# A macaron block: the sixteenth feed-forward's second matrix with one Strassen level of seven products, attention steps over twelve slots, square sums on ScalarE

## The reference

```
x = x + 0.5 * ffn(layernorm(x))
x = x + attention(layernorm(x))
x = x + 0.5 * ffn(layernorm(x))        # the same W1, W3, W2

ffn(x):   hidden = silu(x @ W1.T) * (x @ W3.T)      # 512 -> 2048
          hidden = fwht(hidden)                     # Walsh-Hadamard over 2048
          out = hidden @ W2.T                       # 2048 -> 512
attention(x): rmsnorm, q, k, v by a ternary matrix; 16 heads of 32;
          per chunk of 128 tokens: decayed causal scores, times v,
          plus q times a state carried from chunk to chunk;
          rmsnorm twice, ternary projection
```

## Time and profile before

| | |
|---|---|
| median of 3 runs | 2327.85 us (2327.58 to 2328.8) |
| span of the profiled execution | 2325.7 us |
| PE busy | 2319.4 us |
| DVE busy | 1245.2 us |
| ACT busy | 728.1 us |
| POOL busy | 113.1 us |
| matmuls recorded | 12687 |

### The profile page before, as it was taken

The page is one execution under the profiler, slowest core; times in us unless marked ns, Lnnn a source line. Parts: engine busy times, 40 slices in busy tenths (PEclk is TensorE's granted clock), DMA queues, the critical chain, the costliest instruction groups (busy, mean ns, idle before and its releaser), DMA issues.

```text
span 2325.7 us, 32208 instructions
## 1 busy us (share of the span) xinstructions
PE 2319.4 (100%) x12687; PEld 1105.1 (48%) x12687; DVE 1245.2 (54%) x2484; ACT 728.1 (31%) x1323; POOL 113.1 (5%) x106
## 2 busy tenths in 40 slices
PE   9999999999999999999999999999999999999999
PEld 5444444444444444444444444444444544444444
DVE  7678465655565446546553556545564455455312
ACT  7646133223322332233223322332233323331211
POOL 0290000000000000000000000000000000000000
PEclk9999999999999999999999999999999999999999
DMA  9866533331333214232241214321433124131200
GB/s 244 223 164 170 145 86 75 95 98 32 100 69 105 62 36 113 75 93 50 54 137 43 60 55 114 98 57 32 127 66 104 40 59 96 36 91 37 72 19 19
DMA packets 318086, 200.83 MB, mean 86 GB/s; under 512 B 250096, under 2 KB 274928, under 8 KB 314096
## 3 DMA queue, kind: packets, MB, share of 16 engines
q1 hardware_dynamic: 317504, 197.99, 33.1%
q10 hardware_dynamic: 432, 0.79, 0.1%
HBM read 87.04 MB, written 56.10 MB: 62 GB/s over the span
## 4 chain that ended last, share of the span: by engine, by line
PE 99%; DVE 1%; ACT 0%; DMA 0%; issue 0%; ACTq 0%; DVEq 0%
PE l_bank L1557 28%; PE d_bank L1577 28%; PE g_bank L1557 28%; PE a_bank L1621 4%; PE a_bank L1598 2%; PE a_bank L1676 2%; PE a_bank L1632 1%; PE a_bank L1660 1%; PE a_bank L1646 1%; PE a_bank L1614 1%; PE a_bank L1666 0%; PE a_bank L1662 0%; PE d_bank L1522 0%; DMA xin<-in_L_attn_x_dram 0%; PE a_bank L1522 0%
## 5 line engine op out<-in xcount | busy, mean ns | idle before, releaser
L1577 PE MATMUL d_bank<-w2t,work 128*128 128x512 f16 x2940 | 671.8, 379 | 0.0
L1236 DVE SCALAR_TENSOR_TENSOR work<-l_bank,l_scale,work 128x512 f32<-128x512 f32 x256 | 191.8, 749 | 482.4 <-PE l_bank L1557 482.1
L1577 PEld LDWEIGHTS d_bank<-w2t,work 128*128 128x128 f16 x2940 | 283.7, 98 | 328.7
L1557 PE MATMUL l_bank<-xt,w3t 128*128 128x512 f16 x1536 | 352.4, 379 | 0.0
L1557 PE MATMUL g_bank<-xt,w1t 128*128 128x512 f16 x1524 | 349.7, 379 | 0.0
L939 ACT CAST work<-work 128x512 f16<-128x512 f32 x232 | 143.3, 618 | 562.1 <-DVE work L1236 561.2
L1557 PE MATMUL g_bank<-work,w1t 128*128 128x512 f16 x1344 | 308.4, 379 | 0.0
L1557 PE MATMUL l_bank<-work,w3t 128*128 128x512 f16 x1344 | 308.3, 379 | 0.0
L920 ACT ACTIVATE work<-g_bank,g_scale 128x512 f32<-128x512 f32 x256 | 175.3, 685 | 354.2 <-PE g_bank L1557 351.4
L1557 PEld LDWEIGHTS l_bank<-xt,w3t 128*128 128x128 f16 x1536 | 148.8, 98 | 176.6
L1557 PEld LDWEIGHTS g_bank<-xt,w1t 128*128 128x128 f16 x1524 | 147.3, 98 | 171.9 <-issue 0.8
(11 more groups left out here) (256 smaller groups left out, 1881.4 us busy)
## 6 DMA issues: line engine op xcount, KB each, us to landing
work<-parts_dram SPq DMA_DIRECT2D x192, 128.0 KB, 2.8
x_dram<-work SPq DMA_DIRECT2D x16, 1024.0 KB, 4.2
work<-x_dram SPq DMA_DIRECT2D x11, 1024.0 KB, 6.9
parts_dram<-q_parts SPq DMA_DIRECT2D x32, 256.0 KB, 2.0
parts_dram<-k_parts SPq DMA_DIRECT2D x32, 256.0 KB, 2.2
norm_dram<-cent SPq DMA_DIRECT2D x32, 256.0 KB, 2.0
w2t<-in_L_ffn_W_dram SPq DMA_DIRECT2D x31, 256.0 KB, 3.6
xin<-in_L_attn_x_dram SPq DMA_DIRECT2D x7, 1024.0 KB, 7.4
```

The costliest lines, as they stand in the source:

```text
L1236: nc.vector.scalar_tensor_tensor(out=hfull, in0=l_bank[:], scalar=l_scale[:, j:j + 1], in1=gate, op0=ALU.mult, op1=ALU.mult).then_inc(hful ...
L1557: ins = nc.tensor.matmul(dst[:], wt[:, wp, k, P * j:P * (j + 1)], src[:, xp, k, :], start=(k == 0 and wp == xp), stop=(k == KT - 1 and wp ...
L1577: ins = nc.tensor.matmul(d_bank[t][:], parts[:, hp, P * t:P * (t + 1)], w2t[:, j, wp, :], start=(j == 0 and hp == wp), stop=(j == HT - 1 a ...
```

## The change

Numbers and layouts first. The constant `FAST = 15` names the first feed-forward that is done the new way, so it is the sixteenth alone. The token operands `xt` and `yt` are laid out in two halves of 256 tokens, so the ordinary gate and lin matmuls of all feed-forwards but n = 1 read their 512 tokens as two runs of 256. The hidden values are scaled by a further 1/4. `wproj` loses its own place: it is saved to DRAM during n = 1 (`projsave`) and loaded over the place of `qs` for each batch (`projload`, 8 slots ahead of `proj`); `qT`, `lam_t`, `ident` and others move into the work area.

In the sixteenth, `hgate` and `hlin` make hidden tiles p and p + 8 for 256 tokens into the two halves of a bank. VectorE forms the four 128 x 128 blocks (2 hidden tiles x 2 token tiles), and sums of them; with them there are seven left operands, `combos`. The seven right operands are blocks and sums of blocks of W2; the sums are made once, in the fifteenth feed-forward (`w2sums`), one of four into `w2t` itself, three into DRAM, from where they are streamed for each pair (`w2stream`). `hdown` multiplies, seven products of three matmuls with 256 columns. `hout` and `hend` combine the seven results and the residual on ScalarE, VectorE and GpSimd.

```diff
+                    for e, tile in enumerate((p, p + PAIRS)):
+                        for k in range(KT):
+                            for wp, xp in ((0, 0), (0, 1), (1, 0)):
+                                ins = nc.tensor.matmul(dst[:, HALF * e:HALF * (e + 1)], wt[:, wp, k, P * tile:P * (tile + 1)],
+                                                       f.x[:, s_half, xp, k, :], start=(k == 0 and wp == xp),
+                                                       stop=(k == KT - 1 and wp == 1))
...
+                elif step == "hdown":
+                    pe.wait_ge(lo_ready, tiles_before(n) + HT * s_half + 2 * p + 2)
+                    pe.wait_ge(w2_streamed[q % 2], 16 * (q // 2 + 1))
+                    products = ((0, w2t[:, p, :, left], d_bank[0], left, True),
+                                (4, extra[:, :, 2], d_bank[0], right, False),
+                                (6, extra[:, :, 0], d_bank[1], left, True),
+                                (3, w2t[:, p, :, right], d_bank[2], right, True),
+                                (1, extra[:, :, 1], d_bank[2], left, False),
+                                (2, w2t[:, p + PAIRS, :, left], d_bank[3], left, True),
+                                (5, w2t[:, p + PAIRS, :, right], d_bank[3], right, False))
+                        for hp, wp in ((0, 0), (0, 1), (1, 0)):
+                            ins = nc.tensor.matmul(bank_m[:, cols], combos[:, q % 2, hp, combo, :], weights[:, wp, :],
+                                                   start=(p == 0 and opens and hp == wp), stop=(p == PAIRS - 1 and hp == 1),
+                                                   skip_group_check=True)
```

The steps of the sixteenth, and where `w2sums` go:

```diff
+                if n == FAST - 1 and j >= 2 and j % 2 == 0:
+                    steps += [("w2sums", j // 2 - 1)]
+            if n == FAST - 1:
+                steps += [("w2sums", PAIRS - 1)]
...
+            for s_half in range(2):
+                for p in range(PAIRS):
+                    steps += [("hgate", (s_half, p)), ("w2stream", PAIRS * s_half + p)] + slots.get(slot, []) + [("hlin", (s_half, p))]
+                    if n == FAST and s_half == 0 and p == 0:
+                        steps += [("begin", n - 1), ("down", HT - 1)] + [("resid", t) for t in range(TT)] + [("begin", n)]
+                    steps += [("hlow", (s_half, p, 0))] + slots.get(slot + 1, []) + [("hlow", (s_half, p, 1))]
+                    if p:
+                        steps += [("hdown", (s_half, p - 1))] + slots.get(slot + 2, [])
+                    elif s_half:
+                        steps += [("hdown", (0, PAIRS - 1)), ("hout", 0)] + slots.get(slot + 2, [])
+                        steps += [("hend", 0), ("resid", 0), ("resid", 1)]
+            if last:
+                steps += [("hdown", (1, PAIRS - 1)), ("hout", 1), ("hend", 1), ("resid", 2), ("resid", 3)]
```

`w2sums` on GpSimd, ScalarE and VectorE:

```diff
+                    pool.wait_ge(d_step, steps_before(FAST - 1) + p + 1)
+                    if p:
+                        pool.wait_ge(w2_sum_lo, 2 * p)
+                    for half_h, j in enumerate((p, p + PAIRS)):
+                        ins = nc.gpsimd.tensor_tensor(wide[:, half_h], w2t[:, j, 0, :], w2t[:, j, 1, :], ALU.add)
+                    link(ins)
+                    link(nc.gpsimd.tensor_tensor(w2_sums[:, 0], w2_sums[:, 1], w2_sums[:, 0], ALU.subtract))
+                    link(nc.gpsimd.tensor_tensor(w2_sums[:, 1], w2_sums[:, 1], w2_sums[:, 3], ALU.subtract))
+                    link(nc.gpsimd.tensor_tensor(w2_sums[:, 3], w2_sums[:, 3], w2_sums[:, 0], ALU.subtract))
+                    nc.gpsimd.tensor_tensor(w2_sums[:, 2], w2_sums[:, 2], w2_sums[:, 3], ALU.subtract).then_inc(w2_differences, 1)
...
+                    act.wait_ge(w2_differences, p + 1)
+                    nc.scalar.copy(w2t[:, p, 0, HALF:D], w2_sums[:, 0]).then_inc(w2_sum_hi, 1)
+                    nc.scalar.copy(streamed[:, p % 2, 0], w2_sums[:, 1:4]).then_inc(w2_sum_hi, 1)
...
+                    nc.vector.tensor_tensor(w2t[:, p, 1, HALF:D], w2_sums[:, 0], w2t[:, p, 0, HALF:D], ALU.subtract).then_inc(w2_sum_lo, 1)
+                    nc.vector.tensor_tensor(streamed[:, p % 2, 1], w2_sums[:, 1:4], streamed[:, p % 2, 0],
+                                            ALU.subtract).then_inc(w2_sum_lo, 1)
```

Attention in slots, relative to a group's first slot `at`, and the batch's tail, relative to its last pv:

```diff
-                    add(slots, at - 6, [("q", (b, g))])
-                    add(slots, at - 5, [("qlow", (b, g)), ("k", (b, g))])
...
+                    add(slots, at, [("kv", (b, g)), ("score", (b, g, 0)), ("sclow", (b, g, 0)), ("state", (b, g))])
+                    add(slots, at + 2, [("score", (b, g, 1)), ("sclow", (b, g, 1))])
+                    add(slots, at + 3, [("pv", (b, g, 0))])
+                    add(slots, at + 4, [("score", (b, g, 2)), ("sclow", (b, g, 2))])
+                    add(slots, at + 5, [("pv", (b, g, 1))])
+                    add(slots, at + 6, [("score", (b, g, 3)), ("sclow", (b, g, 3))])
+                    add(slots, at + 7, [("pv", (b, g, 2))])
+                    add(slots, at + 9, [("pv", (b, g, 3))])
...
+                    add(slots, at - 7, [("q", (b, g))])
+                    add(slots, at - 6, [("qlow", (b, g))])
+                    add(slots, at - 5, [("k", (b, g))])
+                    add(slots, at - 3, [("qspread", (b, g)), ("kspread", (b, g))])
+                    end = at + 9
-                    add(slots, end + 11 + t, [("proj", (b, t))])
+                    add(slots, end + 9 + t, [("proj", (b, t))])
+                add(slots, end + 1, [("projload", b)])
-            for at, b in ((19, 3), (109, 4), (253, 5), (364, 6), (461, 7)):
+            for at, b in ((19, 3), (109, 4), (253, 5), (353, 6), (461, 7)):
```

```diff
-                    nc.vector.bn_stats(stat[:, t, :], x2[:, t, :]).then_inc(o_stats, 1)
+                    dve.wait_ge(o_stats, 2 * TT * a + squares_before(t, 0) + 1)
                     nc.vector.tensor_tensor(x2[:, t, :], x2[:, t, :], nw_row[:], ALU.mult).then_inc(o_scaled, 1)
-                    dve.wait_ge(o_scaled, TT * a + (t + 1))
-                    nc.vector.bn_stats(stat[:, TT + t, :], x2[:, t, :]).then_inc(o_stats, 1)
...
+                nc.scalar.activation(squares_out[:, i % 2], x2[:, t, :], ACT.Square, accum_out=sums).then_inc(o_stats, 1)
```

More of the change, by code:

```diff
@@ L289, in feed_forward @@
                 steps += slots.get(base + 3 * j + 2, [])
-                if n == 2 * B - 1 and j == 3:
-                    steps += [("back", batch)]
-            if n == 2 * B - 1:
-                return steps + [("down", HT - 1)] + finish
-            return steps + ([("back", batch)] if which == "ffn2" else [])
+                if n == FAST - 1 and j >= 2 and j % 2 == 0:
+                    steps += [("w2sums", j // 2 - 1)]
+            if n == FAST - 1:
+                steps += [("w2sums", PAIRS - 1)]
@@ L340, in attention_slots @@
                 for t in range(TT):
-                    add(slots, end + 11 + t, [("proj", (b, t))])
-                add(slots, end + 11 + TT, [("keep", b)])
+                    add(slots, end + 9 + t, [("proj", (b, t))])
+                add(slots, end + 1, [("projload", b)])
+                add(slots, end + 9 + TT, [("keep", b)])
                 for t in range(TT):
-                    add(slots, end + 12 + t, [("rows", (("ffn2", b), t))])
-                norm(end + 12 + TT, ("ffn2", b))
+                    add(slots, end + 10 + t, [("rows", (("ffn2", b), t))])
+                norm(end + 9 + TT, ("ffn2", b))
             add(slots, 4, [("early", 3)])
@@ L447, in first_steps @@
                     steps += [("qprep", 10 + 2 * j), ("qprep", 11 + 2 * j)]
+                if j == 5:
+                    steps += [("projsave", 0)]
                 if j < 2:
@@ L456, in macaron_kernel @@
         STEPS = first_steps(SLOTS)
-        for n in range(2, 2 * B):
+        for n in range(2, FAST):
             STEPS += feed_forward(n, SLOTS)
+        for n in range(FAST, 2 * B):
+            STEPS += fast_feed_forward(n, SLOTS)
         def bank_use(step, arg):
@@ L1017, in _ @@
                     nc.scalar.copy(state_parts[:, 0], state).then_inc(state_hi, 1)
+                elif step == "ostat":
+                    a, t = arg
+                    b, _ = filled("pv", (a, GROUPS - 1, TT - 1))
+                    act.wait_ge(a_free[b], copied("pv", (a, GROUPS - 1, TT - 1), b) + 1)
+                    if t == 0:
+                        act.wait_ge(sc_lo, TT * GROUPS * (a + 1))
+                        if a:
+                            act.wait_ge(ln_veps, NORM["o", a - 1] + 1)
+                    square_sum(a, t, 0)
+                    if t:
+                        square_sum(a, t - 1, 1)
+                elif step == "stat" and arg[0] == "o":
+                    square_sum(arg[1], TT - 1, 1)
                 elif step == "score":
```

408 lines of the change are left out of this document (323 added, 85 removed).

## The result

The changed kernel takes 2336.49 us (median of 5, 2335.08 to 2337.1) against 2327.85: ratio 1.0036, 95% interval 1.0024 to 1.0048. It is slower by 8.6 us, where 6.4 were forecast (2334.2, range 2329 to 2340).

What follows compares the result with a forecast made beforehand. TensorE, busy 2319.4 of 2325.7 us, bounds the kernel. Terms 0.7 (matmuls and end) + 3.2 + 1.9 + 0.6 + 0.3 - 0.3 = 6.4 us give span 2332.1, time 2334.2 us; range 2329.0 to 2340.0.

Steps and rivals of the forecast that it cites:

- Matmuls: Sixteenth feed-forward: 576 matmuls of 512 columns become 1104 of 256 at 109.2 ns, saving 3.8 us.
- D: Rival: fourteen feed-forwards reading tokens in two runs of 256 pay 1 ns per matmul, 5.4 us: 2339.6; chance 0.05.
- E: Rival: 256-column matmuls keep more than 109 ns, so the change doesn't save: +3.8, 2338 us; chance 0.03.
- The end: Kernel's end: TensorE stands 1.8 us before the last `hdown`, output chain longer, 10.2 against 6.29 us: +3.9.
- The sums: Fifteenth feed-forward: third `w2sums` queues behind norm "o" on GpSimd, Silu comes late, TensorE stands: +3.2 us.
- Rival A: Third sum in the fifteenth is not late, TensorE never stands there: 2331.0 us, not slower; chance 0.28.
- rival C: GpSimd at its contended price, 8.2 instead of 5.7 us in the third sum: 2336.7 us; chance 0.1.
- The early q: Attention: first group's `q` in slot 7 waits for its last transposition: +1.9 first batch, +0.6 third, 0.3 others.
- That 0.3: Attention: allowance for early `q` waits in the other six batches, 0.3 us (0 to 1.5).
- The recovered 0.3: Attention over twelve slots: a few tenths of small waits won back, -0.3 us.
- the reload of `wproj` and the new spacing: Attention: `wproj` reloaded eight slots ahead booked at 0; key and query spreads together before the scores 0 (0 to 1).
- rival B: Clock falls to 1.2 GHz in the fifteenth's 3.2 us wait, costing another 2.6: 2336.8 us; chance 0.12.

Runs made afterwards that it cites:

- store_later: Changed kernel with first `q` back, sums re-placed, end rearranged, and 1 MB store and load sent behind three norm "o" transpositions: 2326.2 us, ratio 0.9993.
- q_back: Changed kernel with the first head group's `q` moved back from slot 7 to slot 8 of its batch: 2331.88 us, ratio 1.0019.
- no_strassen: Changed kernel with the sixteenth feed-forward done like the others and no sums of weights, attention changes kept: 2333.28 us, ratio 1.0023.
- early_q_only: Kernel before with only the first group's `q` of each batch moved from slot 8 to slot 7: 2331.51 us, ratio 1.0014.
- attention_back: Changed kernel without the new feed-forward and its sums, first `q` back in slot 8, first batch's projections one slot later: 2328.31 us, ratio 1.0001.
- all_back: Changed kernel with first `q` back, first batch's projections one slot later, sums behind tiles 1, 3, ... 15: 2331.36 us, ratio 1.0015.

## Why the prediction was right, and what it missed

**Matmuls: right.** -3.8 forecast, -3.7 measured; rivals D and E fall, 215.8 and 109.2 ns as in the earlier trace rows.

**The end: right mechanism, 0.8 us too dear.** TensorE restarted 3.8 us after the last `hlin` (4.1 forecast), having stood 1.5 (1.8), and VectorE ended at 9.4 (10.2). With the matmuls that makes -0.2 us, where +0.7 was booked.

**The sums: right place, right cause.** Forecast from the end of lin 6: GpSimd starts the third sum at 5.6 and ends at 11.3, TensorE stands 3.2. Measured from 2120.7: 4.8, 10.7, and 2.15. Another 0.63 us before lin 8 were not in the sum: VectorE's part of lin is behind the norm's steps that the same lateness delayed. Together 2.8. Rival A falls; rival C too, since the six additions took 5.9 us. The Trainium skill's 2.6 cycles an element on GpSimd (GPSIMD Engine Reference, section Elementwise: side-by-side cycle accounting), from which the prediction made 1.1 us for 512 columns, doesn't fit this trace: the two additions with f16 inputs took 2.71 us, 1.35 each.

**The early q: right, spread otherwise.** 1.33 (1.9 forecast), 0.41 in the third batch (0.6), and 1.66 in three of the other six, where 0.3 was booked. That 0.3 is the term that was mis-sized: slot 7 leaves the last transposition nothing in several batches, and how late it comes differs from execution to execution (the second batch's wait was 0.40 to 1.08 us in the six profiles with the early `q`). The recovered 0.3 were 0.7.

**Missed: the projection, +1.65.** The prediction costed the reload of `wproj` and the new spacing at 0 and never set the new slots of norm "o" and `proj` beside each other. Before, a tile's transposition was six slots ahead of its projection; now it is four, and in the first batch all of them come behind the 2 MB sent at the third feed-forward's end, where three were ahead of it. SyncE's queue in the kernel before (L729 are the transpositions, L645 and L648 the 2 MB):

```profile
435.02 1.24 SPq L729 DMA_TRANSPOSE zt<-cent  x1
...
437.25 1.24 SPq L729 DMA_TRANSPOSE zt<-cent  x1
...
440.98 1.25 SPq L729 DMA_TRANSPOSE zt<-cent  x1
...
443.15 0.32 SPq L645 DMA_DIRECT2D x_dram<-work  x1
443.52 0.43 SPq L648 DMA_DIRECT2D xin<-in_L_attn_x_dram  x1
443.99 3.77 SPq L729 DMA_TRANSPOSE zt<-cent  x1
```

One slot later, the wait only moved to the next gate; store_later, at the four slots of the change, has none, so the order in the queue was the cause.

**Open: 1.4 us between the profiled execution and the median.** The profiled execution shows no fall of the clock in mid-kernel and took 2335.08, 0.9 above the forecast; the four others took 2335.59 to 2337.1, with a mean clock of 0.999. No profile shows where the clock fell in them, and 0.999 needs no fall in mid-kernel: the profiled execution of store_later reads it too, without one. Two things can make the 1.4, and no run tells them apart. One is rival B, which the forecast gave 0.12 at 3.2 us of standing and a price of 2.6: q_back shows it behind the same wait, at 1.7 us, in some of its executions and not in others. The other is waits on DMAs that vary: all eleven executions of no_strassen have a mean clock of 1.000, so none has such a fall, and they still spread over 3.3 us.

**Open: the start, +0.5.** TensorE's first transposition starts at 11.28 in the kernel before and 11.59 in early_q_only, which share the old layout, and at 11.5 to 12.0 in the kernels with the new one. VectorE's statistics of the last part of `x` begin at 7.74 us instead of 7.24, because that part lands later, though ScalarE's queue issued it at 1.7 us in both. attention_back is 0.4 us above the kernel before, within its interval; more can't be said.

In sum, the terms in it came out at -0.2, +2.8 and +2.7 (forecast +0.7, +3.2, +2.5), and what was not in it at +1.65, +0.5 and +1.4. That the profiled execution lies only 0.9 us above the forecast is partly luck: the terms were 1.1 us too dear together, which hid half of the projection and the start. Around the span it was 1.8 us, where the prediction had added 2.15; so the 7.5 of the table, 1.4 and -0.35 make the 8.6 measured.

## What to carry to other kernels

Where TensorE is busy all the time, list for each moved step the distance to what it needs, in slots, before and after, and what else the same queue carries in between. Neither loss of attention was an operation added: the first `q` came too soon after its transposition, and norm "o", three slots later in its batch, came behind 2 MB in the queue. Steps that are closer together cost nothing once that order is turned round. A step that makes its engine wait for a slow one costs nothing or several microseconds depending only on what stands ahead of the slow engine's part, so look for a place between the other users of that engine. And in a kernel whose TensorE never stands, count a wait of 2 us or more twice: once for itself and once for the clock that may fall behind it.

## What the runs showed of the hardware

- TensorE's granted clock fell from 2.4 to 1.2 GHz in mid-kernel behind a single wait. In the profiles taken, waits of 1.0 to 2.1 us behind the start were followed by the full clock; of two of 2.13 and 2.15 us at the same gate, the first by half of it and the second not; one of 2.63 by the full clock, and all six from 2.74 us on by half. The fall cost 1.4 to 3.0 us more; behind a wait of 3.14 it was 1.6 in one profile and 2.9 in another. (In all_back's profile the clock also reads 0.50 from 12.0 to 15.4 us, in the preparation, and in no other profile.)
- The cost of a wait on a DMA differs from execution to execution, and so do the times: with the early `q` and the projection waiting, no_strassen spread over 3.3 us in 11 executions, all with a mean clock of 1.000; attention_back, with one such wait left, over 1.1.
- One queue: behind a store and a load of 1 MB each, SyncE needed 3.1 to 4.4 us to issue a transposition that otherwise took 1.24.
